# A graph-attention and expert layer on one core: the residual moves from TensorE to GpSimd and VectorE, the first norm's statistics to ScalarE

## The reference, cut to what matters

```python
x = x + gnn(layernorm(x), adj, ...)
x = x + ffn(layernorm(x), ...)

def gnn(x, adj, ...):            # x: 8 x 1024 x 128, four heads of 32
    q, k, v = x @ Wq.T + bq, x @ Wk.T + bk, x @ Wv.T + bv
    scores = clip(q . k / sqrt(32), -10, 10), masked by adj to -10
    attn = softmax(scores within each chunk of 128 keys)
    out = sum over chunks of attn @ v, then @ Wo.T + bo
    out = out + x                 # the residual of this change
    return normalise(out) * gamma + beta

def ffn(x, ...):                  # each token through its two best of eight experts, added
    ...
```

## Time and profile before

| | |
|---|---|
| median of 3 runs | 728.84 us (728.39, 728.84, 732.42) |
| the profiled execution | 730.68 us, of which the span in the trace is 728.9 us |
| PE, DVE, POOL, ACT busy | 691.0, 605.4, 563.2, 503.5 us |
| busiest group | `clip` on DVE, 128 times 2.29 us |

### The profile page before, as it was taken

How to read it: one execution, slowest core, us unless ns; L and a number is a source line. 1 busy time by engine, 2 the same in 40 slices (tenths; PEclk the granted TensorE clock), 3 DMA queues, 4 the chain that set the end, 5 groups by cost and what they waited for, 6 DMA issues and landing times.

```text
span 728.9 us, 17234 instructions
## 1 busy us (share of the span) xinstructions
PE 691.0 (95%) x5510; PEld 362.8 (50%) x5510; DVE 605.4 (83%) x1387; ACT 503.5 (69%) x1017; POOL 563.2 (77%) x616
## 2 busy tenths in 40 slices
PE   8988999999999999999999999989889999999994
PEld 6322233333333323333333333323378899999994
DVE  4789989999999999999999999999897656555552
ACT  4755577787777778677787777666677567667662
POOL 8659586988889898988989889898776776555553
PEclk9998999999999999999999999999999999999997
DMA  7541010010111101111010010014241254333400
GB/s 262 190 130 30 1 30 16 15 45 30 37 38 30 45 16 45 38 38 44 16 45 23 24 45 15 30 37 125 60 129 57 96 154 127 99 95 95 111 28 2
DMA packets 47960, 45.44 MB, mean 62 GB/s; under 512 B 6981, under 2 KB 42576, under 8 KB 47872
## 3 DMA queue, kind: packets, MB, share of 16 engines
q1 hardware_dynamic: 41888, 31.60, 15.1%
q0 software_dynamic: 5984, 12.74, 5.0%
HBM read 27.73 MB, written 18.34 MB: 63 GB/s over the span
## 4 chain that ended last, share of the span: by engine, by line
PE 69%; DVE 15%; issue 7%; ACT 5%; DMA 1%; POOL 1%; DVEq 1%; SPq 1%; POOLq 0%; ACTq 0%
PE scores_ps L454 15%; PE ctx_ps L466 11%; PE scores_ps L630 10%; PE z_ps L473 9%; DVE e L1006 9%; PE ctx_ps L656 5%; PE z_ps L656 5%; ACT x_rows L783 3%; PE job_ps L502 2%; PE job_ps L529 2%; PE job_ps L493 2%; PE job_ps L565 2%; PE job_ps L514 1%; PE job_ps L564 1%; PE scores_ps L616 1%
## 5 line engine op out<-in xcount | busy, mean ns | idle before, releaser
L778 ACT ACTIVATE e<-e 128x2048 f32<-128x2048 f32 x128 | 245.1, 1915 | 145.3 <-DVE e L1006 145.3
L1006 DVE SCALAR_TENSOR_TENSOR e<-scores_ps,bound_mem 128x2048 f32<-128x2048 f32 x128 | 293.2, 2291 | 27.7 <-PE scores_ps L454 22.1
L882 ACT ACTIVATE e<-scores_ps,bound_mem 128x128 f32<-128x128 f32 x364 | 104.4, 374 | 51.0 <-PE scores_ps L630 50.4
L1510 POOL DMA_INDIRECT out<-e,near x91 | 91.1, 1002 | 61.6 <-DVE e L1230 48.7
L473 PE MATMUL z_ps<-e,one_column 128*32 128x512 f32 x1024 | 134.7, 597 | 0.0
L1491 POOL TENSOR_TENSOR ctx_part<-ctx_part,z_inv 128x1024 f32<-128x1024 f32 x60 | 115.7, 1929 | 23.2 <-DVE z_inv L1022 23.2
L1503 POOL TENSOR_TENSOR ctx_sum<-ctx_sum,ctx_part 128x512 f32<-128x512 f32 x90 | 115.4, 1282 | 8.4 <-POOL ctx_sum L1503 0.9
L630 PE MATMUL scores_ps<-e,bound_mem 128*128 128x128 f32 x728 | 97.0, 276 | 4.0 <-ACT e L853 2.1
L1014 DVE STREAM_TRANSPOSE ctx_part<-ctx_ps 128x512 f32<-128x512 f32 x128 | 90.3, 706 | 1.6 <-PE ctx_ps L466 1.6
L630 PEld LDWEIGHTS scores_ps<-e,bound_mem 128*128 128x128 f32 x728 | 88.5, 192 | 5.6 <-ACT e L853 3.9
L1465 POOL DMA_INDIRECT sorted_rows<-x_rows,slot x64 | 63.6, 994 | 19.3 <-issue 16.4
(11 more groups left out here) (188 smaller groups left out, 1011.6 us busy)
## 6 DMA issues: line engine op xcount, KB each, us to landing
near<-sorted_rows SPq DMA_DIRECT2D x91, 130.0 KB, 2.1
near<-in_x SPq DMA_DIRECT2D x16, 256.0 KB, 2.8
bound_mem<-in_adjT SPq DMA_DIRECT2D x4, 1024.0 KB, 9.0
x_post<-in_x SPq DMA_DIRECT2D x16, 256.0 KB, 2.7
sorted_rows<-pad_row SPq DMA_DIRECT2D x1, 3640.0 KB, 15.1
out<-e,near POOLq DMA_INDIRECT x91, 2.3
sorted_rows<-x_rows,slot POOLq DMA_INDIRECT x64, 2.6
bound_mem<-in_w SPq DMA_DIRECT2D x1, 1024.0 KB, 5.4
```

The costliest lines, as they stand in the source:

```text
L778: nc.scalar.activation(every, every, ACT.Exp, scale=SCORE_SCALE).then_inc(exp_done, 1)
L882: nc.scalar.activation(e_flat[:, h_at:h_at + P], scores_ps[:, i % 2, k * P:(k + 1) * P], ACT.Gelu, bias=part_flat[:, bias_at:bias_at + 1]) ...
L1006: dve.scalar_tensor_tensor(out=e[:, s % E_RING], in0=scores_ps[:], scalar=-CLIP, in1=to, op0=ALU.max, op1=ALU.min).then_inc(clipped, 1)
L1510: nc.gpsimd.indirect_dma_start(out=out_rows, out_offset=bass.IndirectOffsetOnAxis(ap=near_u[:, id_at:id_at + 1], axis=0), in_=e_flat[:, at ...
```

## The change

- `project` no longer transposes the residual into the bank: its product starts the bank. The output bias becomes a row (`bo_all`, 128 wide) made once. POOL adds it to the first norm's output in row form (`add_bias`, into `xn_bo`), once per block, between `scale(u-1, 4)` and the additions after it. DVE adds `xn_bo` to the projected bank in step 3, after that step's clip and turn (`add_residual`, into `residual` in SBUF). `square_proj`, still at the end of step 2 in ACT's order, and `normalise_proj` read `residual` and wait for it.
- ACT's second copy (`add_output_bias`) is gone; `keys` waits for the first copy.
- From block 3 on the first norm's sums and squares are taken by ACT (`sum_x` in step 4, `square_x` in step 5), not by DVE. POOL makes the variance in `root_both` with one more small instruction, and the root now waits for the mean's instruction.
- One of the four products of `values` is issued in step 5, behind the ranks, the others stay in step 6.
- ACT's `drain_k` stands ahead of step 4's exponentials, not behind them. DVE's `find_places` moves from step 3 to 4. The rings of loaded tiles and of results in the expert part shrink by one slot each.

```diff
             def keys(v):
-                if v == 0:
-                    pe.wait_ge(xnT_ready, 1)
-                else:
-                    pe.wait_ge(xnT_bo_ready, v + 1)
+                pe.wait_ge(xnT_ready, v + 1)
...
             def project(v, tiles=range(TILES)):
...
-                pe.wait_ge(xnT_bo_ready, v + 1)
                 for t in tiles:
                     cols = slice(t * P, (t + 1) * P)
-                    pe.transpose(job_ps[1][:, cols], xnT_bo[:, v % 4, cols], ident[:])
-                    ins = pe.matmul(job_ps[1][:, cols], ctxT[:, cols], wo_centred[:], start=False, stop=True,
-                                    skip_group_check=True)
+                    ins = pe.matmul(job_ps[1][:, cols], ctxT[:, cols], wo_centred[:], start=True, stop=True)
...
                     if j == 6 and u > 0 and is_block(u + 2):
-                        values(u + 2)
+                        values(u + 2, range(1, TILES))
...
                     if j == 5 and is_block(u - 3):
                         rank(u - 3)
+                    if j == 5 and u > 0 and is_block(u + 2):
+                        values(u + 2, range(1))
...
+            def sum_x(v):
...
+                for t in range(TILES):
+                    ins = nc.scalar.activation(unused[:, t, :], x_in[:, v % 2, t, :], ACT.Copy, scale=-1.0 / D,
+                                               accum_out=l["minus"][:, t, :])
+                ins.then_inc(l["s_mv"], 1)
...
+            def square_x(v):
...
+                    ins = nc.scalar.activation(unused[:, t, :], x_in[:, v % 2, t, :], ACT.Square, bias=l["minus"][:, t, :],
+                                               accum_out=l["mv"][:, t, 1:2])
...
             def square_proj(v):
                 need(act, x2_ready, v)
                 need(act, var2_ready, v)
-                act.wait_ge(proj_filled, v + 1)
+                act.wait_ge(residual_ready, v + 1)
...
                 for j in range(CHUNKS):
                     s = u * CHUNKS + j
+                    if j == 4 and u > 0 and is_block(u + 2):
+                        drain_k(u + 2)
                     exponentials(s)
...
-                    if j == 4 and u > 0 and is_block(u + 2):
-                        drain_k(u + 2)
+                    if j == 4 and is_block(u + 3):
+                        sum_x(u + 3)
+                    if j == 5 and is_block(u + 3):
+                        square_x(u + 3)
...
+            def add_residual(v):
+                dve.wait_ge(proj_filled, v + 1)
+                dve.wait_ge(xn_bo_ready, v + 1)
+                need(dve, n2_ready, v)
+                dve.tensor_tensor(residual[:], job_ps[1][:].rearrange("p (t d) -> p t d", d=D), xn_bo[:, v % 4], ALU.add)\
+                    .then_inc(residual_ready, 1)
...
+                    if j == 3 and is_block(u - 2):
+                        add_residual(u - 2)
...
             for k in range(SLOTS):
                 if k == 1:
+                    add_residual(14)
                     scale_last(4)
...
+            def add_bias(v):
+                need(pool, residual_ready, v - 3)
+                pool.wait_ge(ln["1"]["s_out"], v + 1)
+                if v == 0:
+                    pool.wait_ge(bias_ready, 1)
+                nc.gpsimd.tensor_tensor(xn_bo[:, v % 4], xn[:, v % 2], bo_all[:].to_broadcast([P, TILES, D]), ALU.add)\
+                    .then_inc(xn_bo_ready, 1)
```

More of the change, by code:

```diff
@@ L162, in graph_transformer_layer @@
         xnT = near[:, 5 * SEQ:6 * SEQ].rearrange("p (a n) -> p a n", a=2)
-        xnT_bo = sb("xnT_bo", [P, 4, BLOCK])
+        xn_bo = sb("xn_bo", [P, 4, TILES, D])
+        residual = sb("residual", [P, TILES, D])
         q_last, k_last = sb("q_last", [P, BLOCK]), sb("k_last", [P, SEQ])
@@ L488, in keys, with values @@
             def keys(v):
[L489 to L492 removed]
+                pe.wait_ge(xnT_ready, v + 1)
                 pe.matmul(k_ps(v)[:], w_proj[:, W_K, :], xnT[:, v % 2, :], start=True, stop=True)\
                     .then_inc(k_filled, 1)
[L496 removed]
+            def values(v, tiles=range(TILES)):
                 pe.wait_ge(k_ready, v + 1)
[L498 to L500 removed]
+                for t in tiles:
                     cols = slice(t * P, (t + 1) * P)
                     ins = pe.matmul(v_ps(v)[:, cols], xnT[:, v % 2, cols], w_proj[:, W_V, :], start=True, stop=True)
[L503 removed]
+                if TILES - 1 in tiles:
+                    ins.then_inc(v_filled, 1)
             def queries(v):
@@ L534, in rank @@
                 pe.wait_ge(one_hot_ready, v + 1)
-                need(pe, n2_ready, done(v + 1))
+                need(pe, residual_ready, done(v + 1))
                 to = job_ps[1][:, 0:(TILES + 1) * NP].rearrange("p (t n) -> p t n", n=NP)
@@ L788, in normalise_x @@
                 need(act, xnT_filled, v - 1)
+                need(act, xn_bo_ready, v - 1)
                 normalise(ln["1"], v, xn[:, v % 2], x_in[:, v % 2])
-            proj_rows = job_ps[1][:].rearrange("p (t d) -> p t d", d=D)
+            def sum_x(v):
+                l = ln["1"]
+                act.wait_ge(l["s_shift"], v)
+                act.wait_ge(l["s_var"], v)
+                act.wait_ge(x_loaded[v % 2], 16 * (v // 2 + 1))
+                for t in range(TILES):
[3 more added lines that the diff above has]
+            def square_x(v):
+                l = ln["1"]
+                act.wait_ge(l["s_mv"], v + 1)
+                for t in range(TILES):
+                    ins = nc.scalar.activation(unused[:, t, :], x_in[:, v % 2, t, :], ACT.Square, bias=l["minus"][:, t, :],
+                                               accum_out=l["mv"][:, t, 1:2])
+                ins.then_inc(l["s_var"], 1)
             def square_proj(v):
@@ L795, in square_proj @@
                 need(act, var2_ready, v)
-                act.wait_ge(proj_filled, v + 1)
+                act.wait_ge(residual_ready, v + 1)
                 for t in range(TILES):
-                    ins = nc.scalar.activation(n2[:, t, :], proj_rows[:, t, :], ACT.Square, scale=1.0 / float(np.sqrt(D)),
+                    ins = nc.scalar.activation(n2[:, t, :], residual[:, t, :], ACT.Square, scale=1.0 / float(np.sqrt(D)),
                                                accum_out=mean_square[:, t, :])
@@ L804, in normalise_proj @@
                 for t in range(TILES):
-                    ins = nc.scalar.activation(n2[:, t, :], proj_rows[:, t, :], ACT.Copy, scale=rstd2[:, t, :])
+                    ins = nc.scalar.activation(n2[:, t, :], residual[:, t, :], ACT.Copy, scale=rstd2[:, t, :])
                 ins.then_inc(n2_ready, 1)
@@ L895, in _ @@
             drain_q(0)
-            add_output_bias(0)
+            act.wait_ge(bias_filled, 1)
+            nc.scalar.activation(bo_all[:, 0, :], z_ps[:, D:2 * D], ACT.Copy).then_inc(bias_ready, 1)
             normalise_x(1)
@@ L1274, in _ @@
                             find_best(u - 3)
-                        if j == 3:
+                        if j == 4:
                             find_places(u - 3)
-                        if j == 4:
                             mark_pair(u - 3)
-                    if j == 4 and is_block(u + 3):
-                        begin_statistics_x(u + 3, range(1 if u else 0, TILES))
                     if j == 5 and is_block(u - 2):
                         begin_statistics_x2(u - 2)
-                    if j == 6 and is_block(u + 3):
-                        end_statistics(ln["1"], u + 3)
                     if j == 6 and is_block(u - 2):
@@ L1336, in _ @@
                     turn_sum(15)
+                if k == 8:
+                    add_residual(15)
                 if k == 9:
@@ L1444, in root @@
                 roots[l["name"]] += 1
-                nc.gpsimd.tensor_tensor(l["minus"][:], l["mv"][:, :, 0:1], minus_one[:, 0:TILES], ALU.mult)\
-                    .then_inc(l["s_minus"], 1)
+                if l["name"] == "1" and v >= 3:
+                    nc.gpsimd.tensor_scalar(l["var"][:], l["mv"][:, :, 1:2], 1.0 / D, LN_EPS, ALU.mult, ALU.add)\
+                        .then_inc(l["s_minus"], 1)
+                    pool.wait_ge(l["s_minus"], roots[l["name"]])
+                else:
+                    nc.gpsimd.tensor_tensor(l["minus"][:], l["mv"][:, :, 0:1], minus_one[:, 0:TILES], ALU.mult)\
+                        .then_inc(l["s_minus"], 1)
                 nc.gpsimd.tensor_tensor(l["rstd"][:], l["var"][:], minus_half[:, 0:TILES], ALU.pow)\
@@ L1522, in _ @@
                 prepare_bound(0, c)
+            for v in range(3):
+                add_bias(v)
             for u in range(BLOCKS):
@@ L1537, in _ @@
                     scale(u - 1, 4)
+                if u > 0 and is_block(u + 2):
+                    add_bias(u + 2)
                 if is_block(u - 1):
```

32 lines of the change are left out of this document (11 added, 21 removed).

## The result

The changed kernel takes **772.3 us** (median of 4 runs, 771.67 to 775.29), beside 729.5 us for the kernel before (4 runs): a ratio of 1.0587, interval 1.0569 to 1.0605. Forecast were 755 us, with a range up to 769. The sign and the mechanism came as forecast; the time lies 3 us above the range. The profiled execution took 775.29 us, its span is 773.5 against 728.9.

A forecast was written before the change was run, and what follows sets the result against it. PE was taken to bound the kernel, with DVE and POOL close behind. 12 blocks at 2.25 us more gave +27, block 1 -2, expert part +1: 728.84 + 26 = 755 us, range 741 to 769.

The forecast's parts named there:

- block 1: First clip's 1.39 us wait for POOL's mask goes, with part of what followed: 2 us less.
- the chain: Blocks 2 to 13: late residual delays ACT's squares, exponentials, `drain_xnT`, PE's `keys` and POOL; 2.25 us more a block.
- the wait at the turning: Step 0: PE idle about 0.7 us ahead of the turning, because POOL's shift for `normalise_x2` is late.
- PE's own path: With PE idle 1.8 us ahead of `keys`, next step 1 at 33.0; POOL's later 33.65 decides.
- Ends: Outside the 12 full blocks: block 1 gains 2 us, the expert part loses 1, blocks 14 and 15 nothing.
- the clock as a rival: Half clock behind the `keys` gap costs 1 us more a block; 767 us in all 12 blocks; chance 0.2.
- The rival's middle case: Clock falls behind `keys` in half of the 12 blocks: 761 us; the clock rival's chance is 0.2.
- the ends behind block 13: Expert part: POOL has block 14's squares 2.4 us later, costing 1 us; blocks 14 and 15 otherwise nothing.
- worth nothing: Values' product moved: 0.27 us longer in step 5, 0.27 shorter in step 6, no net effect.
- POOL's shorter path: `root_both` is in time, so PE's 33.0 decides, or 32.8 with a cheaper addition: 745 us; chance 0.15.
- Faster: PE never stands still for `keys`; 0.3 us saved in 12 blocks, 2 in block 1: 723 us; chance 0.08.
- the saving that the prediction counted for transposes and tile: Steps 1 and 2: four transposes and DVE's statistics tile gone, some 0.3 us a block were nothing else touched.

The follow-up runs named there:

- e5: Changed kernel plus eight unused identity products on PE in its idle time ahead of `keys`: 761.4 us, 1.0431 of the kernel before.
- e4: Kernel before, with only `square_proj` made to wait for step 3's turn: 754.4 us, 1.0313 of the kernel before.
- e3: Changed kernel with DVE's `add_residual` moved from step 3 to step 2, behind its turn: 739.7 us, 1.0111 of the kernel before.
- e1: Changed kernel with POOL's `add_bias(0)` moved ahead of two of block 0's masks: 764.1 us, 1.0445 of the kernel before.
- e9: e7 with the four products of the values together again in step 6: 725.7 us, 0.9932 of the kernel before.
- e10: Kernel before with only the values' products split, one in step 5, three in step 6: 731.9 us, 1.0021 of the kernel before.
- e7: e6 plus gate maxima in step 3, `add_bias` behind the context's last addition, block 14's residual between scalings: 727.5 us, 0.9955 of the kernel before.
- e8: Kernel before with only the first norm's statistics on ACT and POOL, rings one slot smaller: 728.2 us, 0.9968 of the kernel before.
- e6: Changed kernel with both `add_bias(0)` ahead of the last two masks and `add_residual` in step 2: 733.5 us, 1.0057 of the kernel before.

## Why the prediction was right in direction and wrong in size

By its own steps, counted from step 1's scores at 230.34 in the block shown:

| step | forecast | measured |
|---|---|---|
| residual there | 13.0 | 12.85 |
| squares start | 13.05 | 12.97 |
| POOL starts on them | 14.27 | 14.34 |
| `keys`, and PE's idle time ahead of it | 16.6, 1.8 | 16.58, 1.79 |
| the shift that `normalise_x2` needs | 31.2 | 30.92 |
| next step 1 | 33.65 | 33.45 |
| blocks 2 to 13, clock up | +27 us | +24.7 (e5) |
| the same, falls of the clock | none | +8.1 |
| block 0 | none | +10.0 |
| block 1 | -2 | -2.1 |
| from block 14 on | +1 | +3.6 |

- **Right: the chain.** That `square_proj` kept its place while its input moved behind step 3's clip, was read from the diff and the order on ACT, and each time on the way came out within 0.3 us (the wait at the turning was 0.39 us, not 0.7). e4 and e3 show it from both sides: that wait put into the kernel before costs 22 us, taken out of the changed one it gives nearly all back. In the blocks without a fall of the clock POOL decided as forecast, with 33.45 us over PE's own path of 31.40 + 1.79 = 33.19; with a fall PE's path, 34.8 us by the same count, decided. The addition took 0.65 us, near the 0.7 taken from the turn's row. The squares took 1.37 us to POOL's first use, not 1.22; the estimate from the Trainium skill ("ScalarE: Activation LUTs", section "What ACT_TABLE_LOAD costs"), 293 ns for each, agrees with the rows of the squares, which read SBUF now (0.29 to 0.31 us).
- **Wrong: "Ends", block 0.** The step that failed first. The list of ends began with block 1. The change holds the wait, `need(act, xn_bo_ready, v - 1)` in `normalise_x` (a line that the excerpt of the diff leaves out), and POOL's order has `add_bias(0)` behind the masks; the prediction costed `add_bias` by its 1.29 us on POOL and never asked who waits for it. e1: 8.3 of block 0's 10.0 us, 8 us of the median.
- **Wrong: the clock as a rival, not as part of the sum.** The gap was sized at 1.8 us and came at 1.79 and 1.88, between the two waits that the trace of before had. The fall came in six of twelve blocks, each behind 1.88. The rival's middle case, half of the blocks, is what happened; its 6 us measured 8.1. The trace of before could not say whether 1.8 us is enough for a fall, and the sum put that term at nothing.
- **Too small: the ends behind block 13.** Block 14, costed at nothing for lack of `keys`, still has the late residual: DVE's third-norm statistics stood 1.07 us for POOL's rows, PE 1.76 us for the clip after them; in e3 that step takes 3.63 us again, not 4.76. In the expert part ACT's squares of block 14 waited for DVE's addition, PE 2.19 us, and its products ran near half clock behind that (granted clock 0.58; 1.83 us for a usual 1.16).

```profile
524.59 0.88 DVE L984 BATCH_NORM_STATS2 ln_stats<-x_rows 128x6 f32<-128x128 f32 x4 [1.07 <-POOL x_rows L1497]
...
573.53 0.31 ACT L814 ACTIVATE n<-residual 128x128 f32<-128x128 f32 x1 [0.79 <-DVE residual L1090]
...
575.02 1.83 PE L626 MATMUL scores_ps<-e,bound_mem 128*128 128x128 f32 x8 [2.19 <-ACT e L858]
```

- **Wrong, but hidden: "worth nothing" for the moved product.** It costs 0.2 us a block where PE is the path (e9, e10). In the changed kernel POOL's chain covers it.
- **Of the other rivals**, POOL's shorter path (745) is out, since POOL's path did decide. "Faster", which asked for the addition ahead of step 3's clip, is what e7 and e9 build: e9's blocks are 0.3 us shorter than before, the saving that the prediction counted for transposes and tile; e8, with the tile gone and the transposes kept, saves none of it. The transposes alone were not run. In place of the forecast gain of 6 us e9 has 4.6 against the kernel before beside it: the blocks from 14 on keep 1.4 us of the loss.

The forecast's 26 us, plus 10 for block 0, 8 for the clock and 2.6 for the rest behind block 13, less 2.3 by which the waits were oversized, are 44.3; the spans differ by 44.6. The medians differ by less, 42.8, since the profiled execution of the changed kernel was the slowest of its four, 3 us above their median.

## What to carry to other kernels

When an input is made later, follow every consumer that keeps its place in its engine's order: what is queued behind it moves too, and that price (here 22 us) is paid even where no work is added. For each new semaphore also ask about the first time round, where the producer stands behind set-up work; a wait for a free buffer is a wait like any other. A change that loses 6% may hold parts worth keeping: with six of its instructions or groups moved, the same work came out 0.7% faster than before.

## What the runs showed of the hardware that was not expected

- **Where the clock fell.** In the changed kernel and e1, PE's waits ahead of `keys` were 1.88 us twelve times, and half clock followed ten times; after ten waits of 1.78 or 1.79 us it followed never. In e4, with waits of 1.75 and 1.66 us in turn, it followed one of the six of 1.75. Two waits of 1.88 in e1, both ahead of its first fall, had none behind them. So the length alone does not settle it, and what else does was not tried.
- **Splitting a group of products cost time.** Two groups of the values' products in place of one took 0.2 us more for the same products (e10 beside e9), with no idle time of PE in the rows around them. Why was not tried.
- **Block 0 differs from execution to execution.** e6 and e7 issue the same instructions up to here. DVE's first mask waits for a DMA of the adjacency, 1.56 us in e6's profile and 2.91 in e7's. Ahead of step 1's scores PE stood 0.37 us in the one, 2.11 in the other, and only in the other did half clock follow, with a step 1 of 4.61 us for 3.62:

```profile
17.08 1.14 PE L457 MATMUL scores_ps<-q_last,near 32*128 32x512 f32 x8 [0.37 <-DVE e L1016]
```

```profile
18.82 1.71 PE L457 MATMUL scores_ps<-q_last,near 32*128 32x512 f32 x8 [2.11 <-DVE e L1016]
```

  With it block 0 takes 35.6 us in e7 and 32.9 in e6. Single times of one kernel here differ by that much (e6 took 732.7 to 736.8 us), so part sums of single profiles are read from block 2 on.
